# Second attention: sixteen maxima first, tile 14's output between their scores, tile 15's after them

## What is computed

```
x = x + xattn0(layernorm(x), ctx)       # 16 heads of 16, softmax, a bias of -0.1*|t - s|
x = x + ffn0(layernorm(x))              # 1024 experts by product keys (top 8) + a dense silu part
x = x + xattn1(layernorm(x), ctx)       # relu(q), relu(k), relu(v); softmax(q.k/4) v
x = x + ffn1(x)                         # 8 experts, 2 for each token
```

## Time and profile before

| what | us |
|---|---|
| three runs | 1198.83, 1201.91, 1202.25 (median 1201.91) |
| the profiled execution | 1192.25 |
| its span, first to last instruction | 1190.4 |
| mean granted TensorE clock in it | 0.943 of full speed |
| PE / DVE / ACT / POOL busy | 1044.9 / 799.8 / 644.5 / 491.1 |

### The profile page before, as it was taken

One profiled execution on the slowest core, in us unless ns is written; L12 is line 12 of the kernel. 1 busy time (PEld: TensorE's weight loads), 2 busy tenths in 40 slices (PEclk: granted clock), 3 DMA queues, 4 the chain that ended last, 5 costly groups with the idle time before them and its releaser, 6 DMA issues.

```text
span 1190.4 us, 16994 instructions
## 1 busy us (share of the span) xinstructions
PE 1044.9 (88%) x5486; PEld 651.2 (55%) x5486; DVE 799.8 (67%) x2005; ACT 644.5 (54%) x859; POOL 491.1 (41%) x526
## 2 busy tenths in 40 slices
PE   8899999998767989999999688999899888799991
PEld 3344344433446878778777563434334334588881
DVE  7767686886788787787786246778677856244443
ACT  3456555565546776676775503656455561355550
POOL 6568786884304424425434402113123336122220
PEclk9799999999989999999999987999898898899996
DMA  8845968558999000000003300475354328222226
GB/s 247 259 116 168 291 214 272 172 176 250 250 236 230 2 1 1 1 1 1 1 28 81 103 21 28 125 204 140 93 170 107 88 66 330 77 68 71 73 63 212
DMA packets 74202, 149.89 MB, mean 126 GB/s; under 512 B 7823, under 2 KB 44577, under 8 KB 72580
## 3 DMA queue, kind: packets, MB, share of 16 engines
q1 hardware_dynamic: 61380, 98.80, 31.4%
q0 software_dynamic: 10800, 47.63, 11.2%
q10 hardware_dynamic: 1936, 2.36, 0.7%
HBM read 73.14 MB, written 76.25 MB: 125 GB/s over the span
## 4 chain that ended last, share of the span: by engine, by line
PE 56%; DVE 23%; ACT 8%; issue 5%; POOL 4%; DMA 4%; SPq 1%; DVEq 0%; ACTq 0%; POOLq 0%
PE ps L1232 14%; PE ps L1362 8%; DVE negmax L1753 8%; PE ps L1329 5%; PE ps L1343 4%; PE ps L1305 4%; PE ps L1314 3%; PE ps L1560 3%; PE ps L1537 3%; PE ps L1523 3%; PE ps L1371 2%; PE ps L1677 1%; DVE moe_w L2079 1%; DVE hl L1758 1%; DMA moe_w<-in_w 1%
## 5 line engine op out<-in xcount | busy, mean ns | idle before, releaser
L1753 DVE TENSOR_REDUCE negmax<-ps 128x1 f32<-128x512 f32 x512 | 321.9, 683 | 76.3 <-PE ps L1329 75.9
L1024 ACT ACTIVATE pt<-ps 128x1024 f32<-128x1024 f32 x256 | 257.4, 1026 | 140.0 <-PE ps L1343 139.0
L1329 PE MATMUL ps<-sk,sq 56*128 56x512 f32 (+1 forms) x512 | 159.8, 449 | 32.9 <-DVE negmax L1753 23.0
L1362 PE MATMUL ps<-pt,v_aug 128*32 128x512 f32 x1024 | 145.7, 634 | 1.7 <-POOL pt L756 1.4
L1343 PE MATMUL ps<-sq,sk 57*128 57x512 f32 (+1 forms) x512 | 130.7, 496 | 3.5 <-issue 1.4
L1329 PEld LDWEIGHTS ps<-sk,sq 56*128 56x128 f32 (+1 forms) x512 | 72.8, 197 | 87.6 <-DVE negmax L1753 71.1
L756 POOL TENSOR_TENSOR pt<-pt,near 128x256 f32<-128x256 f32 x128 | 92.1, 728 | 67.2 <-ACT pt L1024 66.7
L1343 PEld LDWEIGHTS ps<-sq,sk 57*128 57x128 f32 (+1 forms) x512 | 51.4, 192 | 102.3 <-issue 75.4
L927 POOL DMA_INDIRECT expert_out<-yo,dest x39 | 38.1, 977 | 119.0 <-ACT yo L1198 107.0
L841 POOL TENSOR_TENSOR w_first<-w_first,moe_w 128x1024 f32<-128x1024 f32 x16 | 38.1, 2380 | 106.4 <-DVE pt L2071 105.7
L1523 PE MATMUL ps<-sel,hl 128*128 128x512 f32 x256 | 72.6, 416 | 7.0 <-DVE pt L2071 6.2
(11 more groups left out here) (319 smaller groups left out, 2020.3 us busy)
## 6 DMA issues: line engine op xcount, KB each, us to landing
expert_rows<-zero SPq DMA_DIRECT2D x3, 5586.0 KB, 57.5
expert_weights_split<-wst POOLq DMA_DIRECT2D x8, 2048.0 KB, 9.0
qk_rows<-hl SPq DMA_DIRECT2D x30, 512.0 KB, 3.0
sk<-qk_rows SPq DMA_DIRECT2D x62, 192.0 KB, 4.9
sq<-qk_rows SPq DMA_DIRECT2D x62, 192.0 KB, 4.5
moe_w<-in_w POOLq DMA_DIRECT2D x16, 512.0 KB, 6.9
wexp<-expert_weights_split POOLq DMA_DIRECT2D x16, 512.0 KB, 4.5
wexp<-expert_weights_split SPq DMA_DIRECT2D x4, 2048.0 KB, 17.1
```

The lines of the kernel that those rows point to most:

```text
L1024: act.activation(pt[:, 4 * (U % 2) + 2 * half:4 * (U % 2) + 2 * half + 2, :], ps[:, 2 + 2 * half:4 + 2 * half, :], ACT.Exp, scale=(BIAS, S ...
L1329: pe.matmul(ps[:, job.bank, :], sq[r, pair, t * P:(t + 1) * P], sk[r, pair, :], start=True, stop=True).then_inc(s_job, 1)
L1362: ins = pe.matmul(ps[32 * j:32 * j + 32, OBANK, :], v_aug[:, b % 2, c, HG * g + j, :], pt[:, 4 * (U % 2) + j, :], start=(c == 0), stop=(c ...
L1753: dve.tensor_reduce(negmax[:, n % 2, col:col + 1], src, AX, ALU.max, negate=True).then_inc(s_jd, 1)
```

## The change

The second attention starts at step -4 and has only 16 scores ahead of step 0; the other 12 move into steps 0 to 8, by the table `MORE` that the first attention uses. Tile 14's output is cut into three parts (`finish_part`), behind the four scores of steps -4, -3 and -2; tile 15's whole output stands behind the turn of the first sixteen maxima, at the end of step -1. `EARLY` gets six banks. `add_pair` is split into `pair_sum` (the addition that frees bank 7) and `pair_rest`; the rest of pair 6 moves behind the first maxima's copy, the sum of pair 7 behind that, and its rest behind the reductions of step 0. Batch 1's preparation is k at steps 0 and 1, xt at 2 and 3, q at 4 and 5, v at 6 and 7.

```diff
@@ -34,7 +34,7 @@
 LASTU = B * NU
 JBANK = (0, 1, 7)
 AHEAD = (0, 1, 7, 2, 3, 4)
-EARLY = (0, 1, 3)
+EARLY = (0, 1, 3, 2, 4, 5)
 OBANK = 6
 FF = 1024
@@ -129,7 +129,7 @@
 Job = namedtuple("Job", "n kind b i by done bank after")
 EMPTIED_BY_ACT = ("xt", "v", "on", "gt", "wr", "gb", "ns")
 PREPARE = {-22: ("xt", 0), -21: ("xt", 1), -20: ("k", 0), -17: ("k", 1), -16: ("q", 0), -15: ("q", 1), -13: ("v", 0), -12: ("v", 1)}
-PREPARE_SECOND = {-17: ("xt", 0), -16: ("xt", 1), -15: ("k", 0), -14: ("k", 1), -13: ("q", 0), -12: ("q", 1), -11: ("v", 0), -10: ("v", 1)}
+PREPARE_SECOND = {-16: ("k", 0), -15: ("k", 1), -14: ("xt", 0), -13: ("xt", 1), -12: ("q", 0), -11: ("q", 1), -10: ("v", 0), -9: ("v", 1)}
 FINISH = {21: ("on", 0), 22: ("on", 1), 23: ("wo", 0), 24: ("wo", 1)}
 ROUTE = {25: ("gt", 0), 26: ("gt", 1), 27: ("gl", 0), 31: ("rk", 0)}
 FIRST = (("xt", 0), ("xt", 1), ("k", 0), ("k", 1), ("q", 0))
@@ -143,14 +143,14 @@
 SPLIT_OUT = (8, 15, 20, 27, 32, 39, 44, 51)
 LOAD_RAW = (15, 16, 22, 28, 34, 40)
 BUSY = {LASTU + 5: 2, LASTU + 13: 3}
-STEPS = (range(-HG, LASTU + 9), range(-LEAD, LASTU + 18))
+STEPS = (range(-HG, LASTU + 9), range(-HG, LASTU + 18))
 PREPARE_1 = {-18: ("k", 0), -17: ("k", 1), -14: ("xt", 0), -13: ("xt", 1), -12: ("q", 0), -11: ("q", 1), -10: ("v", 0), -9: ("v", 1)}
 PREPARED = ((None, PREPARE_1, PREPARE, PREPARE), (None, PREPARE_SECOND, PREPARE, PREPARE))
 STACKS = (None, 10, 12, 12)
-NEXT_CTX = ((2, -9), (-LEAD, -9))
+NEXT_CTX = ((2, -9), (-HG, -9))
 def attention_jobs():
@@ -189,20 +189,22 @@
                 extra.append((START[U][0], 0, START[U][1]))
             if L == 0 and U in AHEAD_B:
                 extra.append((AHEAD_B[U][0], 0, AHEAD_B[U][1]))
-            more = MORE.get(U, 4) if L == 0 else 4
+            more = MORE.get(U, 4)
             scores = [("s", n // (4 * NU), n % (4 * NU)) for n in range(scored, min(scored + more, 4 * LASTU))]
             scored += more
             for kind, b, i in scores[:2] + extra + scores[2:]:
                 add(U, kind, b, i)
             if U >= 6 and U % 4 == 2 and U - 6 < LASTU:
                 add(U, "ot", (U - 6) // NU, (U - 6) % NU // 4)
-            if L == 0 and U == -1:
-                add(U, "v", 0, 0)
+            if U == -1:
+                if L == 0:
+                    add(U, "v", 0, 0)
                 add(U, "m", 0, 0)
-                add(U, "v", 0, 1)
-            if L == 0 and U == 2:
+                if L == 0:
+                    add(U, "v", 0, 1)
+            if U == 2:
                 add(U, "m", 0, 1)
-            if U % 4 == 1 and L == 0 and 1 < U < LASTU - 3 or U % 4 == 1 and L and 0 <= U + 3 < LASTU:
+            if U % 4 == 1 and 1 < U < LASTU - 3:
                 add(U, "m", (U + 3) // NU, (U + 3) % NU // 4)
         table.append(steps)
     return table, at, n, count
@@ -995,8 +997,8 @@
                     empty(L, job)
                 for U in STEPS[L]:
                     Ug = LASTU * L + U
-                    if L and U in (-5, -3):
-                        weights_copy(NTL - 2 + (U + 5) // 2)
+                    if L and U in (-4, -1):
+                        weights_copy(NTL - 2 + (U + 4) // 3)
                     if L == 0 and U == -2:
                         for s in range(2):
                             first_query_rows(s)
@@ -1400,6 +1402,7 @@
                 else:
                     pe.wait_ge(s_u, RH * NTL)
                     pe.wait_ge(s_pm, RH * NTL)
+                    pe.wait_ge(s_fs, NTL)
                 if L == 0:
                     pe.wait_ge(s_ctx[0], 16)
                     pe.wait_ge(s_wf, 1)
@@ -1416,11 +1419,9 @@
                 if L:
                     pe.wait_ge(s_rowin, 16 * 2)
                 for U in STEPS[L]:
-                    if L and U in (-5, -3):
-                        finish_tile(NTL - 2 + (U + 5) // 2)
                     if L and U == 0:
-                        pe.wait_ge(s_x2, NTL // 2)
-                        emptied_by(last_ahead(1, EARLY[-1]))
+                        for bank in EARLY[2:]:
+                            emptied_by(last_ahead(1, bank))
                     if L and U in BUSY:
                         keep_busy(BUSY[U])
                     if L == 0 and U == 0:
@@ -1433,6 +1434,8 @@
                     keys = 0 <= U < LASTU
                     if keys:
                         scores_by_key(L, U, 0)
+                    if L and U == 0:
+                        pe.wait_ge(s_x2, NTL // 2)
                     for job in scores[0:1]:
                         score(L, job)
                     for job in scores[1:2]:
@@ -1444,6 +1447,8 @@
                         scores_by_key(L, U, 1)
                     for job in scores[2:]:
                         score(L, job)
+                    if L and U < 0:
+                        finish_part(NTL - 2, U + HG)
                     for job in around[0:1]:
                         for part in range(2):
                             extra(L, job, part)
@@ -1454,6 +1459,8 @@
                             turn_out(L, job)
                         if job.kind == "m":
                             turn_max(L, job)
+                    if L and U == -1:
+                        finish_tile(NTL - 1)
                     for job in around[1:2]:
                         for part in range(2):
                             extra(L, job, part)
@@ -1568,13 +1575,18 @@
             pe.wait_ge(s_late, 16 * 8)
             pe.wait_ge(s_sel, 1)
             pe.wait_ge(s_wrl, KC)
+            def finish_part(n, part):
+
+                if part < 2:
+                    turn_weights(n, part)
+                    ff_down(n, part)
+                if part == 2:
+                    add_experts(n, range(EC))
+
             def finish_tile(n):
-                turn_weights(n, 0)
-                ff_down(n, 0)
-                turn_weights(n, 1)
-                ff_down(n, 1)
-                add_experts(n, range(EC))
+                for part in range(3):
+                    finish_part(n, part)
             def first_projection(kind, i):
                 front_free((kind, 0, i))
@@ -1804,11 +1816,14 @@
                     if job.by == "d":
                         empty(L, job)
                 for U in STEPS[L]:
-                    if L and U == -2:
-                        add_pair(NTL // 2 - 1)
                     for job in table[L][U]:
                         if job.by == "d":
                             empty(L, job)
+                    if L and U == -1:
+                        pair_rest(NTL // 2 - 2)
+                        pair_sum(NTL // 2 - 1)
+                    if L and U == 0:
+                        pair_rest(NTL // 2 - 1)
                     if L and U == 1:
                         rstd2_seed(2, 4)
                     if L == 0 and U == -1:
@@ -2090,11 +2105,18 @@
                 own.wait()
                 dve.sem_inc(s_rz, 1)
-            def add_pair(p):
+            def pair_sum(p):
                 b, t = 2 * p // TT, 2 * p % TT
                 dst = x_tok[:, b, t:t + 2, :].rearrange("p t d -> p (t d)")
                 dve.wait_ge(s_yu, 2 * p + 2)
                 dve.tensor_tensor(dst, ps[:, YBANK, :], dst, ALU.add).then_inc(s_x2, 1)
+
+            def add_pair(p):
+                pair_sum(p)
+                pair_rest(p)
+
+            def pair_rest(p):
+                b, t = 2 * p // TT, 2 * p % TT
                 dve.wait_ge(s_x2, p + 1)
                 dve.wait_ge(s_wc, 2 * p + 2)
                 for i in range(2):
@@ -2163,7 +2185,7 @@
                 times_hidden(s, 3)
             row_low("q", 0)
             row_low("q", 1)
-            add_pair(NTL // 2 - 2)
+            pair_sum(NTL // 2 - 2)
             attention(1)
             tile_tables()
```

## The result

The changed kernel takes 1194.58 us at its median, against 1202.19 us before in the same rounds. The ratio is 0.9941 with a 95% interval of 0.9917 to 0.9964, so some 7.1 us are saved (4.3 to 10). 13.5 us were forecast. The time lies outside the forecast's own range (1186.5 to 1191) and at the upper end of the whole range (1183.5 to 1195), and the saving is half of what the sum said. The ratio leaves out two slow executions of the changed kernel (1629.68 us at a mean granted clock of 0.549, and 1204.94 at 0.918); the median is that of all 21. The profiled execution of after took 1186.86 us (span 1185.0), that of before 1192.25 us (span 1190.4).

What follows compares the result with a forecast made beforehand. The prediction took PE to bound the kernel, with waits for VectorE and low clock around the turn between layers. It summed 19.9 - 6.4 = 13.5 us saved, from 1201.91 to 1188.4 us; own range 1186.5 to 1191, whole range 1183.5 to 1195.

Steps and rivals of the forecast that it cites:

- the sum: Second attention: step 0 starts 19.9 us earlier, steps 0 to 8 give back 6.4, so 13.5 us are saved.
- a clock of 0.5 in steps 0 to 2: One of the signs named in advance that would show the forecast wrong, in the second attention's first steps.
- The turn: Between the layers, first score to step 0: tiles 14 and 15 at 7.89 us each, step 0 starts 19.9 us earlier.
- rival 1: The clock falls at waits ahead of the turn or in steps 0 to 2: 6 us lost, 1194.4 us; chance 0.22.
- tile 15 takes 7.9 us: Tile 15's output, behind the turn of the maxima, was expected at full clock: 7.89 us instead of 9.55.
- Steps 0 to 8: Second attention's steps with 12 more scores: 46.8 us forecast, 6.4 more than the 40.33 before.
- the half of pair 7's rest: Step 1: half of VectorE's 1.90 us taken as on the path, between bounds of nothing and 1.90.
- rival 3: The gain is handed back through waits for DMA queues at step 9 or step 4: 1199 us; chance 0.10.
- Rival 2: The gain is larger, from cheaper steps and no clock drop ahead of tile 15: 16 to 18 us saved; chance 0.12.
- rival 4: Slower: the clock stays at 0.50 from step 0 to step 8, 33 us more, 1221 us; chance 0.04.
- It starts at 686.32 as before: The turn's first score was taken as unmoved, the added wait for the last silu costing nothing.
- The base: The saving of 13.5 us was taken from the timed runs' 1201.91 us, giving 1188.4, not from the profiled 1192.25.

Runs made afterwards that it cites:

- fill_wait: The changed kernel with two useless matmuls in PE's 2.43 us wait ahead of the maxima's turn; ratio 0.9843 against before, median 1199.75 us.
- busy_steps: The changed kernel with one useless matmul in step 0 and one in step 1, ahead of the fifth score; ratio 0.9883 against before, median 1187.64 us.
- whole_14: The changed kernel with tile 14's output in one piece behind step -2's scores instead of in three parts; ratio 0.9988 against before.
- rep_after2: The changed kernel run again unaltered, its third trace; steps 0 to 8 took 54.98 us, 23.9 us of low clock in them.
- rep_before4: The kernel before run again unaltered, its fifth trace; feed-forward to tile 13 took 358.24 us.
- rep_before5: The kernel before run again unaltered, its sixth trace; feed-forward to tile 13 took 357.52 us.

## Why the prediction was half right

The sum was 19.9 - 6.4 = 13.5 us saved. The traces show 18.5 - 10.5 = 8.1 on average (from unrounded values) and the timed runs 7.1, with an interval of 4.3 to 10 that leaves 13.5 out. The rebuilt order and its waits were right; the granted clock was not. The prediction had named a clock of 0.5 in steps 0 to 2 as a sign that it was wrong, and three of four traces of the changed kernel have low clock in step 1.

**The turn held.** Forecast 21.7 us from first score to step 0, measured 23.16. Six banks, tile 14 between the scores and tile 15 over the maxima's rows did what the sum said; the wait ahead of the maxima was 2.43 for 2.1. The 1.5 us more is the low stretch in tile 15 (1.69 by fill_wait), which the prediction had named and left to rival 1. That tile 15 takes 7.9 us was wrong: 9.6. The sum had no term for this, though before's own tile 15 showed the stretch.

**Steps 0 to 8 held at full clock.** Forecast against after, step by step: 5.6 and 5.36, 7.2 and 7.44, 4.6 and 4.43, 4.0 and 3.58, 5.7 and 5.57, 6.0 and 5.83, 10.45 and 10.45, 3.2 and 3.55; in sum 46.8 and 46.2. Step 1 came out right to 0.24 us, but the half of pair 7's rest in it was a midpoint between two bounds, and no run says how much of the rest is on the path: that is in part luck. No queue handed anything back: PE waits for no DMA from step 0 to 900 us in after, so rival 3's waits didn't come. That the two profiled executions are equal to 0.01 us from step 9 on is luck, since this stage takes 421.2 to 429.5 us in the ten traces of the two kernels. Rival 2's larger gain in steps 5 to 8 isn't there.

**The step that failed is rival 1 in size, place and chance.** The sum put the cost of the clock in steps 0 to 8 at nothing (46.8 us), and rival 1 said: 6 us, in steps 0 to 2, with chance 0.22, against it that "the k projections [...] keep PE busy for 2 us of steps 0 and 1". The runs show 8.8 us, in steps 1 to 4, in two of four traces of the changed kernel, and 0.8 in a third, which makes 50.8 on average. The k products didn't protect: the clock fell inside them. It also stayed low through `values` and scores until the q products were nearly done; that was priced only in rival 4, with 33 us for all nine steps and a chance of 0.04, and nothing stood between the two. The sum took as the likeliest case one that holds about half of the time, and gave it for the median. busy_steps bears the place out: with PE kept busy in steps 0 and 1 they took 46.5 us each time. Why the clock falls in some executions and not in others, and why it stays low so long, is open.

**A reading that was wrong.** Rival 1 says that the clock of 0.67 in 688 to 692 us stood "when PE worked at VectorE's pace of one score in 0.6 us, not when it stood still". But PE was idle for 2.69 us until 689.74, and before's trace has the granted clock at 1.00 up to 689.3 and at 0.50 from 689.4 on: it fell while PE still stood idle. That work at such a pace can bring the fall is shown by whole_14 instead, where PE had waited 0.48 us in a row at most, and by step 1 of rep_after2. The rows that rival 1 cites don't show it.

**The balance.** Means over the traces of the table (six of before, four of after):

| stage | before | after | saved |
|---|---|---|---|
| start to feed-forward | 318.1 | 317.3 | 0.8 |
| feed-forward to tile 13 | 358.15 | 361.86 | -3.7 |
| tile 13 | 12.60 | 14.20 | -1.6 |
| first score to step 0 | 41.68 | 23.16 | 18.5 |
| steps 0 to 8 | 40.31 | 50.78 | -10.5 |
| step 9 to end | 425.69 | 422.05 | 3.6 |
| span | 1196.5 | 1189.4 | 7.2 |

The rebuilt stretch saves 8.1 us on average, not 13.5: 1.5 are lost in the turn, and 4.0 in the steps (50.78 for 46.8), since two traces of four take 8.8 more than after's. Together with the rest this gives 7.2 us, beside the 7.1 of the timed runs. So close an agreement is luck: the spans of either kernel's traces scatter with a standard deviation of 5 us. The three largest other rows nearly cancel (-3.7 - 1.6 + 3.6), but they are not all noise. The stretch from the feed-forward to tile 13 has the same instructions in both kernels; yet it had 41.0 us of low clock, and took 361.7 to 362.2 us, in all four traces of after and nine of its ten variants, and in one of six of before. Chance alone would give so uneven a split in about 2 of 1000 cases, and in 24 of 1000 for the two kernels alone (four of four against one of six). The question came from looking at the first traces; rep_before4 and rep_before5 were run for it and stand on the side of a cause in the changed program. Which it is stays open, since nothing in that stretch was altered. The prediction took whatever lies ahead of the first score as unmoved ("It starts at 686.32 as before"); after's starts at 693.47.

**The base.** Adding the saving to the median of the runs and not to the profiled execution was right: that one, at 1192.25, was among before's lowest times.

## What to carry to other kernels

Where a change leaves PE waiting for banks behind an engine that sets its pace, price the low clock with a chance of its own, and for longer than until the next dense products: it lasted 3.4 us here in two traces and 23.9 in four. Take several traces and compare them by stage before you trust a difference: two executions of one kernel differed by 8.8 us in nine steps with the same instructions. One matmul of no use in each of the two steps cost 0.3 us in all, and none of five traces then had low clock there. Cutting a dense tile into parts between scores gives VectorE its time and spares PE low clock; doing it in one piece instead (whole_14) left hardly any of this change's gain.
